# Waits of the weight-ternarising stage of a transformer layer on Trainium2: what the weight loads and the Abs pass wait for

## The chip, the cores and the metric

The kernel runs on all 8 cores of one Trainium2 chip, one batch entry of 2048 tokens on each. Each core has five engines with instruction streams of their own (TensorE, VectorE, ScalarE, GpSimd and SyncE, in the profile PE, DVE, ACT, POOL and SP) and 16 DMA engines. The metric is the device time in microseconds of the slowest core.

## The reference, cut to what matters

```python
def _bitlinear(x, w_latent):
    scale = clip(mean(abs(w_latent), axis=1, keepdims=True), 1e-05, None)
    tern = clip(round(w_latent / scale), -1.0, 1.0)
    w = w_latent + stop_gradient(tern - w_latent)
    return x @ (w * scale).T
h = _bitlinear(x, w_fc) + gate * (x @ v.T @ fast_b.T @ u.T)
r = maximum(h, 0.0)
return _bitlinear(r * r, w_proj)          # w_fc [4096, 1024], w_proj [1024, 4096]
# around it, x [8, 2048, 1024]:
x = x + attn_block(layernorm(x), ...)     # linear attention and a GELU MLP
x = x + ffn(layernorm(x), ...)            # the function above
```

Each row of w_fc and w_proj is thus replaced by its signs where the absolute value is above half of the row's mean absolute value, and by 0 elsewhere; the row's scale is applied later.

## The kernel before, in words

The program is written engine by engine with explicit semaphores. `block.sync`, `block.scalar`, `block.vector`, `block.tensor` and `block.gpsimd` append the given function's instructions to that engine's stream; no scheduler moves them. `b.inc` lets an instruction raise its engine's counter (`"t"`, `"v"`, `"s"` for TensorE, VectorE, ScalarE), `b.wait(engine, name, value)` makes an engine wait for a value, and `b.cnt[name]` is the count emitted so far. `b.dma` (L52) issues a transfer. Loads are issued by SP under the name `"ld"`, whose four semaphores are used in turn, and spills by GpSimd under `"gq"`, with two semaphores; each transfer also waits for the one before it on its own semaphore. Every engine's stream is in order.

The stages are: attention, output projection and GELU MLP (until about 3700 us), the statistics of the second layernorm, then the **weight stage** (from L1362 on, ends at L1562), a small stage that transposes `u` (L1603), and the second FFN over four groups of 512 tokens.

In the weight stage w_fc is taken in 32 stripes of 128 rows (loop at L1384), w_proj in 8 stripes of 128 rows by 4096 columns (loop at L1457).

A **w_fc stripe** `si` goes so. SP loads it (512 KB) in two halves into one of two buffers, `wfbuf[si % 2]` (L1388). ScalarE takes the absolute values into `ab_s` and their sum into `sc_fc` (L1399); in the profile this is a table load, the ACTIVATE and a read of the accumulator. VectorE forms scale and thresholds (four small instructions, L1408 to L1416), compares with the upper threshold into `ab_s` (L1419) and with the lower one into `tern_b` (L1422), which is the last reader of the buffer. TensorE transposes 8 blocks into `ps_trf` (L1432), VectorE copies them into one of two `evac_fc` buffers (L1444), and GpSimd spills these 256 KB to `spill_fc` in DRAM (L1450), as rows of 128 bf16 values. The tile names in the profile are `ph` for all f32 buffers of the stage (`wfbuf`, `ttf4`, `ab_s`, `abs4`) and `ph7b` for `tern_b` and the evacuation buffers.

A **w_proj stripe** `j` (2 MB) is loaded in four quarters into the single buffer `ttf4` (L1461), with rows of 1024 f32 values. ScalarE writes its absolute values to `abs4` (L1474). VectorE compares four quarters (L1496, L1499); the last of these eight instructions is the last reader of `ttf4`. Then four times: 8 transposes (L1512), a copy to one of two `evac_pj` buffers (L1523), a spill of 256 KB to `spill_pj` (L1530). The third copy waits for the first spill, whose buffer it takes, and the fourth for the second.

What the loads wait for is set by hand. The w_fc load waits for `vprev`, all VectorE work emitted before it, which is the copy of the stripe before:

```python
vprev = b.cnt["v"]
def _(sy, si=si, wb_=wb_, vprev=vprev):
    b.wait(sy, "v", max(vprev, v_ln0b))
```

The w_proj load waits for all VectorE work and for all spills emitted before it:

```python
b.wait(sy, "v", vprev)
b.wait(sy, "gq", gprev)
```

ScalarE waits only for the load (`"ld"`). Lines of helpers: DMAs are recorded at L57, waits at L81 and L83.

Of the kernel before, what the change touches and what calls it, by code (L numbers as in the profile page):

```python
# [85 lines left out]
def build_program(tap=None, phases=99):  # L86
# [29 lines left out]
    with contextlib.ExitStack() as ctx:  # L116
# [34 lines left out]
        b = Bld(nc, block)  # L151
# [25 lines left out]
        def emit_tap(src_ap):  # L177
            cv, cs, ct = b.cnt["v"], b.cnt["s"], b.cnt["t"]

            def _(gp):  # L180
                b.wait(gp, "v", cv)
                b.wait(gp, "s", cs)
                b.wait(gp, "t", ct)
                b.dma(gp, "gq", out=tap_d[0:src_ap.shape[0], 0:src_ap.shape[-1]],
                                   in_=src_ap)
                b.wait(gp, "gq")
            block.gpsimd(_)
# [3 lines left out]
        def _(sy):  # L191
            off = 0
            for nm in ["bo", "b2", "g1", "be1", "g2", "be2", "b1"]:
                nch = PC[nm][1]
                b.dma(sy, "ld", out=A_t[0:nch, off:off + 128],
                                   in_=bias_d[nm].rearrange("(c p) -> c p", p=128))
                off += 128
            b.dma(sy, "ld", out=gate_b[:], in_=gate_d.partition_broadcast(128))
            b.dma(sy, "ld", out=fbT[:], in_=fb_d)
            b.dma(sy, "ld", out=A_t[0:16, 1024:2048], in_=vw_d)  # L200
            b.dma(sy, "ld", out=ident[:], in_=ident_d)
        block.sync(_)
        ld_par = b.cnt["ld"]

        def _(v):
            v.memset(ones_c[:], 1.0)
            v.memset(epsc[:, 0:1], EPS_OUT)
            v.memset(epsc[:, 1:2], EPS_IN)
            b.inc(v.memset(ones_r[:], 1.0), "v", 1)
        block.vector(_)  # L210

        def _(sc):
# [4 lines left out]
        with nc.psum_tensor("ps_m", [128, 128], F32) as ps_m:  # L217
            off = 0
            for nm in ["bo", "b2", "g1", "be1", "g2", "be2", "b1"]:
                nch = PC[nm][1]  # L220
                vprev = b.cnt["v"]
# [20 lines left out]
            vprev = b.cnt["v"]  # L242
# [11 lines left out]
            for k in range(ND):  # L254
                vprev = b.cnt["v"]
# [21 lines left out]
        with nc.sbuf_tensor("ph0", [128, 5376], F32) as P0, \  # L277
# [9 lines left out]
            for si in range(NT):  # L287
                xb = xt[si % 2]
                wv_, ws_ = done[si - 2] if si >= 2 else (0, 0)
# [6 lines left out]
                ldv = b.cnt["ld"]  # L296
# [26 lines left out]
            vv = b.cnt["v"]  # L323
# [8 lines left out]
            sv = b.cnt["s"]  # L332
# [11 lines left out]
            for si in range(NT):  # L344
                xb, zb = xt[si % 2], zt[si % 2]
                wv_ = v_ev if si >= 2 else 0
# [5 lines left out]
                ldv = b.cnt["ld"]  # L352
# [727 lines left out]
        with nc.sbuf_tensor("ph5", [128, 9728], F32) as P5, \  # L1080
# [10 lines left out]
            for g in range(G):  # L1091
# [177 lines left out]
                with nc.psum_tensor(f"ps_sg1_{g}", [1, 512], F32) as psg1, \  # L1269
                     nc.psum_tensor(f"ps_sg2_{g}", [1, 512], F32) as psg2:  # L1270
                    for n in range(ND):
# [9 lines left out]
                        sv = b.cnt["s"]  # L1281
# [22 lines left out]
                    vv = b.cnt["v"]  # L1304
# [9 lines left out]
                    sv = b.cnt["s"]  # L1314
# [50 lines left out]
        v_ln0b = b.cnt["v"]  # L1365
# [14 lines left out]

        with nc.psum_tensor("ps_trf", [128, 1024], BF16) as ps_trf:
            g_fc = [0, 0]
            t_trf = 0
            for si in range(NF):  # L1384
                wb_ = wfbuf[si % 2]
                vprev = b.cnt["v"]

                def _(sy, si=si, wb_=wb_, vprev=vprev):  # L1388
                    b.wait(sy, "v", max(vprev, v_ln0b))
                    for hh in range(2):  # L1390
                        b.dma(sy, "ld", out=wb_[:, hh * 512:(hh + 1) * 512],
                              in_=wfc_d[si * 128:(si + 1) * 128,
                                        hh * 512:(hh + 1) * 512])
                block.sync(_)
                ldv = b.cnt["ld"]

                def _(sc, si=si, wb_=wb_, ldv=ldv):
                    b.wait(sc, "ld", ldv)
                    b.inc(sc.activation(ab_s, wb_, AF.Abs,  # L1399
                                        accum_out=sc_fc[:, si:si + 1]), "s", 1)  # L1400
                block.scalar(_)
                sv = b.cnt["s"]

                def _(v, si=si, wb_=wb_, sv=sv, t_trf=t_trf):
                    b.wait(v, "s", sv)
                    b.wait(v, "t", t_trf)
                    b.wait(v, "v")
                    b.inc(v.tensor_scalar(sc_fc[:, si:si + 1], sc_fc[:, si:si + 1],  # L1408
                                          INV_D, None, ALU.mult), "v", 1)
                    b.wait(v, "v")  # L1410
                    b.inc(v.tensor_scalar(sc_fc[:, si:si + 1], sc_fc[:, si:si + 1],
                                          1e-5, None, ALU.max), "v", 1)
                    b.wait(v, "v")
                    v.tensor_scalar(thr_s[:, 0:1], sc_fc[:, si:si + 1], 0.5,
                                    None, ALU.mult)
                    b.inc(v.tensor_scalar(thr_s[:, 1:2], sc_fc[:, si:si + 1], -0.5,  # L1416
                                          None, ALU.mult), "v", 1)
                    b.wait(v, "v")
                    b.inc(v.tensor_scalar(ab_s, wb_, thr_s[:, 0:1], None, ALU.is_gt),  # L1419
                          "v", 1)  # L1420
                    b.wait(v, "v")
                    b.inc(v.scalar_tensor_tensor(  # L1422
                        tern_b[:, 0:1024],
                        wb_, thr_s[:, 1:2], ab_s, ALU.is_lt, ALU.subtract), "v", 1)
                block.vector(_)
                vv = b.cnt["v"]

                def _(t, vv=vv):
                    b.wait(t, "v", vv)
                    last = None  # L1430
                    for k in range(ND):
                        last = t.transpose(ps_trf[:, k * 128:(k + 1) * 128],  # L1432
                                           tern_b[:, k * 128:(k + 1) * 128],
                                           ident_b[:])
                    b.inc(last, "t", 1)
                block.tensor(_)
                t_trf = b.cnt["t"]

                ev_ = evac_fc[si % 2]

                def _(v, t_trf=t_trf, gw=g_fc[si % 2], ev_=ev_):
                    b.wait(v, "t", t_trf)
                    b.wait(v, "gq", gw)
                    b.inc(v.tensor_copy(ev_, ps_trf[:]), "v", 1)  # L1444
                block.vector(_)
                vv = b.cnt["v"]

                def _(gp, si=si, vv=vv, ev_=ev_):
                    b.wait(gp, "v", vv)
                    b.dma(gp, "gq", out=sfc_d[si].transpose([1, 0, 2]),  # L1450
                                       in_=ev_
                                       .rearrange("p (k c) -> p k c", k=ND))
                block.gpsimd(_)
                g_fc[si % 2] = b.cnt["gq"]

            g_pj = [0, 0]
            for j in range(ND):  # L1457
                vprev = b.cnt["v"]
                gprev = b.cnt["gq"]

                def _(sy, j=j, vprev=vprev, gprev=gprev):  # L1461
                    b.wait(sy, "v", vprev)
                    b.wait(sy, "gq", gprev)
                    for qq in range(4):
                        b.dma(sy, "ld",
                              out=ttf4[:, qq * 1024:(qq + 1) * 1024],
                              in_=wpj_d[j * 128:(j + 1) * 128,
                                        qq * 1024:(qq + 1) * 1024])
                block.sync(_)
                ldv = b.cnt["ld"]  # L1470

                def _(sc, j=j, ldv=ldv):
                    b.wait(sc, "ld", ldv)
                    b.inc(sc.activation(abs4, ttf4, AF.Abs,  # L1474
                                        accum_out=sc_pj[:, j:j + 1]), "s", 1)
                block.scalar(_)
                sv = b.cnt["s"]
# [24 lines left out]
                            ALU.is_lt, ALU.subtract), "v", 1)  # L1502
                block.vector(_)
                vv = b.cnt["v"]

                for q in range(4):
                    def _(t, q=q, vv=vv):
# [28 lines left out]
            gprev = b.cnt["gq"]  # L1536
# [31 lines left out]
        with nc.sbuf_tensor("ph8", [128, 6672], F32) as P8, \  # L1568
# [32 lines left out]
            with nc.psum_tensor("ps_u", [128, 128], F32) as ps_u:  # L1601
                v_prev = v_prep
                for st in range(NF):  # L1603
# [7 lines left out]
                    vv = b.cnt["v"]  # L1611
# [18 lines left out]
            for g in range(G):  # L1630
# [20 lines left out]
                for k in range(ND):  # L1651
# [12 lines left out]
                    vv = b.cnt["v"]  # L1664
# [9 lines left out]
                with nc.psum_tensor(f"ps_lr_{g}", [16, 512], F32) as ps_lr:  # L1674
# [19 lines left out]
                    vv = b.cnt["v"]  # L1694
# [14 lines left out]
                with nc.psum_tensor(f"ps_h2_{g}", [128, 1536], F32) as ps_h2:  # L1709
# [4 lines left out]
                    for i in range(NF):  # L1714
                        ws_ = t_fc[i % 2]
# [7 lines left out]
                        ldv = b.cnt["ld"]  # L1723
# [51 lines left out]
                for half in range(2):  # L1775
                    with nc.psum_tensor(f"ps_y_{g}_{half}", [128, 2048], F32) as ps_y:
# [3 lines left out]
                        ldv = 0  # L1780
                        for i in range(NF):
                            if i % 2 == 0:
# [14 lines left out]
                                ldv = b.cnt["ld"]  # L1797
# [24 lines left out]
                        for jj in range(4):  # L1822
                            j = half * 4 + jj
# [82 lines left out]
```

How the kernel before makes its waits and increments, by code:

```python
    def dma(self, eng, base, out, in_, **kw):  # L52
        j = self.rri[base] % RR[base]
        self.rri[base] += 1
        s = f"{base}{j}"
        self.wait(eng, s)
        instr = eng.dma_start(out=out, in_=in_, **kw)
        instr.then_inc(self.sem[s], 16)
        self.cnt[s] += 16
        self.cnt[base] += 16
        self.snap[base][self.cnt[base]] = tuple(
            self.cnt[f"{base}{k}"] for k in range(RR[base]))
        return self.cnt[base]
# [1 line left out]
    def inc(self, instr, name, n=1):  # L65
        assert name not in self.snap
        instr.then_inc(self.sem[name], n)
        self.cnt[name] += n
        return self.cnt[name]
# [1 line left out]
    def wait(self, eng, name, val=None):  # L71
        if val is None:
            val = self.cnt[name]
        assert val <= self.cnt[name], \
            f"wait {name}>={val} but only {self.cnt[name]} emitted"
        if val == 0:
            return
        if name in self.snap:
            for k, c in enumerate(self.snap[name][val]):
                if c > 0:
                    eng.wait_ge(self.sem[f"{name}{k}"], c)
            return
        eng.wait_ge(self.sem[name], val)
```

## Time and profile before

| | us |
|---|---|
| three runs | 5910.05, 6027.0, 6244.59 (median 6027.0) |
| the profiled execution | 5910.97 |
| its span on the slowest core (core 3) | 5909.4 |
| spans of the 8 cores | 5900.5 to 5909.4 |
| mean granted clock of TensorE, all cores | 0.817 to 0.818 of full speed |
| TensorE busy (matmuls) | 3797.6 (64% of the span) |
| VectorE, ScalarE, GpSimd busy | 1589.7, 1224.8, 165.0 |

Busy times are those of instructions that compute; waiting, branches and the issue of DMAs don't count. The granted clock is a share of full speed: 1.00 is 2.4 GHz, 0.50 is 1.2 GHz. A timeline row gives the start, the duration, the engine with its line, what is written from what, and in brackets how long the engine was idle before and what ended that.

### The profile page before, as it was taken

What the parts mean: (1) busy time and instruction counts of PE and PEld (TensorE: products, weight loads), DVE (VectorE), ACT (ScalarE), POOL (GpSimd) and SP (SyncE); (2) the same over time, 40 slices, a digit from 0 to 9 for tenths busy, and PEclk for the clock granted to TensorE, in tenths of its full rate; (3) what the DMA queues carried; (4) which work ended last, traced back from release to release, by engine and by line L of the source; (5) the groups of instructions that cost most, each with busy time, mean ns of one, the idle gap of its engine ahead of it and who ended that gap; (6) DMA issues with size and microseconds to landing.
All of it is one profiled execution on the core that took longest, in us unless ns stands there. A gap on an engine that the chain in (4) does not pass through costs nothing.

```text
span 5909.4 us, 49644 instructions; the slowest of 8 cores (5900.5 to 5909.4 us)
## 1 busy us (share of the span) xinstructions
PE 3797.6 (64%) x16136; PEld 1605.1 (27%) x16136; DVE 1589.7 (27%) x1972; ACT 1224.8 (21%) x1279; POOL 165.0 (3%) x228
## 2 busy tenths in 40 slices
PE   1266654656965994994995996400013988969697
PEld 1122222222412441341441442000001333323233
DVE  2354555542014102202202201122333213031220
ACT  2034442320021202301301311222110504123050
POOL 0011110000000000000000000000010000000000
PEclk9988877866977996996997997755555999989799
DMA  2233331000002321431431431022221222212122
GB/s 94 93 114 107 105 109 47 1 0 29 0 0 64 93 86 47 89 100 32 100 93 37 96 93 43 18 66 69 75 87 36 54 68 47 61 49 59 50 54 68
DMA packets 655522, 374.36 MB, mean 63 GB/s; under 512 B 548176, under 2 KB 581152, under 8 KB 655280
## 3 DMA queue, kind: packets, MB, share of 16 engines
q1 hardware_dynamic: 635312, 304.06, 19.6%
q0 software_dynamic: 19968, 67.12, 3.4%
q8 instruction: 145, 2.38, 0.2%
q14 instruction: 97, 0.79, 0.1%
HBM read 312.39 MB, written 58.72 MB: 63 GB/s over the span
## 4 chain that ended last, share of the span: by engine, by line
PE 53%; DVE 19%; ACT 10%; DMA 10%; issue 6%; DVEq 1%; SPq 1%; ACTq 0%; POOLq 0%; POOL 0%
PE ps_p L1240 11%; PE ps_h L1178 11%; PE ps_h L1733 8%; PE ps_y L1812 8%; PE ps_wo L949 3%; DMA ph<-x 2%; PE ps_h L1736 2%; DMA ph<-wfc 2%; ACT L587 1%; DVE phwp L578 1%; DVE phwpb L594 1%; PE ps_ctx L902 1%; PE ps_s L991 1%; ACT phwpb L587 1%; PE ps_s L993 1%
## 5 line engine op out<-in xcount | busy, mean ns | idle before, releaser
L1178 PE MATMUL ps_h<-ph5p 128*128 128x512 bf16 x3072 | 682.2, 382 | 54.2 <-DVE ph5p L1140 35.8
L1240 PE MATMUL ps_p<-strB,ph5p 128*128 128x512 bf16 x3072 | 672.5, 382 | 32.4 <-DMA ph5p<-spill_w2p 32.1
L1812 PE MATMUL ps_y<-strB,ph8w 128*128 128x512 bf16 x2048 | 469.9, 388 | 63.3 <-DMA ph8w<-spill_pj 50.7
L1733 PE MATMUL ps_h<-ph8z,ph8w 128*128 128x512 bf16 x2048 | 473.9, 385 | 14.4 <-DMA ph8w<-spill_fc 14.4
L1178 PEld LDWEIGHTS ps_h<-ph5p 128*128 128x128 bf16 x3072 | 296.4, 98 | 439.6 <-issue 103.0
L1240 PEld LDWEIGHTS ps_p<-strB,ph5p 128*128 128x128 bf16 x3072 | 302.3, 99 | 402.6 <-issue 46.6
L501 PE MATMUL ps_v<-strB,ph1zp 128*128 128x512 bf16 x768 | 202.8, 433 | 272.1 <-DVE ph1zp L491 272.1
L1750 ACT ACT_TABLE_LOAD x128 | 164.2, 1283 | 955.2 <-PE ps_h L1736 935.0
L1194 ACT ACT_TABLE_LOAD x128 | 164.2, 1283 | 740.6 <-PE ps_h L1178 740.6
L1812 PEld LDWEIGHTS ps_y<-strB,ph8w 128*128 128x128 bf16 x2048 | 197.7, 99 | 336.9 <-issue 126.8
L501 PE MATMUL ps_q<-ph1qw,ph1zp 128*128 128x512 bf16 x768 | 199.8, 428 | 137.2 <-DVE ph1zp L491 137.2
L1733 PEld LDWEIGHTS ps_h<-ph8z,ph8w 128*128 128x128 bf16 x2048 | 192.2, 99 | 331.0 <-issue 124.9
L1432 PE MATMUL ps_trf<-ident_b,ph7b 128*128 128x128 bf16 x256 | 32.4, 306 | 351.3 <-DVE ph7b L1422 351.3
L1202 DVE CAST strB<-ps_h 128x512 bf16<-128x512 f32 x128 | 88.6, 692 | 526.8 <-ACT ps_h L1194 526.8
L1278 ACT ACT_TABLE_LOAD x32 | 41.1, 1283 | 845.0 <-DVE ph L1258 745.7
L1258 DVE TENSOR_SCALAR ph<-ps_p,pcol 128x512 f32<-128x512 f32 x32 | 21.4, 743 | 717.3 <-PE ps_p L1246 717.3
L949 PE MATMUL ps_wo<-strB,ph3w 128*128 128x512 bf16 x768 | 176.2, 387 | 50.1 <-DVE ph3w L474 31.9
L1761 DVE CAST strB<-ps_h 128x512 bf16<-128x512 f32 x128 | 88.6, 692 | 439.2 <-ACT ps_h L1753 439.2
L1512 PE MATMUL ps_trf<-ident_b,ph7b 128*128 128x128 bf16 x256 | 32.4, 306 | 263.5 <-DVE ph7b L1499 233.7
L501 PEld LDWEIGHTS ps_v<-strB,ph1zp 128*128 128x128 bf16 x768 | 82.1, 108 | 387.7 <-issue 320.7
L501 PE MATMUL ps_k<-strB,ph1zp 128*128 128x512 bf16 x768 | 168.4, 379 | 0.0
L1828 DVE SCALAR_TENSOR_TENSOR ph<-ps_y,scn_pj,strA 128x512 f32<-128x512 f32 x32 | 21.8, 744 | 505.1 <-PE ps_y L1812 505.1
(209 smaller groups left out, 3703.9 us busy)
## 6 DMA issues: line engine op xcount, KB each, us to landing
ph5p<-spill_w1p SPq DMA_DIRECT2D x256, 256.0 KB
ph5p<-spill_w2p SPq DMA_DIRECT2D x256, 256.0 KB
ph8w<-spill_fc SPq DMA_DIRECT2D x128, 256.0 KB
ph8w<-spill_pj SPq DMA_DIRECT2D x128, 256.0 KB
ph<-x SPq DMA_DIRECT2D x32, 512.0 KB
phwp<-w1t SPq DMA_DIRECT2D x32, 512.0 KB
spill_w1p<-phwpb POOLq DMA_DIRECT2D x64, 256.0 KB, 4.5
phwp<-w SPq DMA_DIRECT2D x32, 512.0 KB
```

The source lines that it names most:

```text
L501: last = t.matmul(ps[:, cols], zz[:, k * 128:(k + 1) * 128], ww.rearrange("p (k w) -> p k w", k=ND)[:, k, cols], start=(pi == 0 and k == 0 ...
L587: b.inc(sc.copy(wpb[:, 0:1024], tb), "s", 1)
L949: t.matmul(ps_wo[:, cols], wfn[:, e_, n * 128:(n + 1) * 128], bfn(e_)[:, cols], start=(pi == 0 and e_ == 0), stop=False)
L1178: last = t.matmul(dst, ww[:, k * 128:(k + 1) * 128], aa[:, k, :], start=(pi == 0 and k == 0), stop=(pi == 2 and k == ND - 1))
L1194: b.inc(sc.activation(ps_h[:, 1024:1536], src, AF.Gelu, bias=pc("b1", i)), "s", 1)
L1202: b.inc(v.tensor_copy(B16[:, i * 1024:i * 1024 + 512], ps_h[:, 1024:1536]), "v", 1)
L1240: last = t.matmul(ps_p2[:, n * 512:(n + 1) * 512], ww[:, n * 128:(n + 1) * 128], mm, start=(i == 0 and pi == 0), stop=False)
L1733: t.matmul(dst, fcb[i % 2][:, k * 128:(k + 1) * 128], zz(k), start=(pi == 0 and k == 0), stop=False)
L1736: b.inc(t.matmul(dst, uTg[:, i * 128:(i + 1) * 128], t2T[0:16, :], start=False, stop=True), "t", 1)
L1750: b.inc(sc.activation(bcz[:, 0:512], src, AF.Relu, scale=scn_fc[:, i:i + 1]), "s", 1)
L1761: b.inc(v.tensor_copy(B16[:, i * 1024:i * 1024 + 512], ps_h2[:, 1024:1536]), "v", 1)
L1812: last = t.matmul(ps_y[:, jj * 512:(jj + 1) * 512], buf[:, off + jj * 128:off + (jj + 1) * 128], mm, start=(i == 0 and pi == 0), stop=(i = ...
```

## The change

The order of all instructions stays; the waits of the stage's loads and of its Abs passes are set anew.

- The w_fc load waits for the last comparison (`v_fcg`) and the Abs (`s_fcg`) of the stripe that used the same buffer, two stripes earlier, and no longer for the copy of the stripe before.
- The w_proj load waits for the last comparison of the stripe before (`v_pjt`; for the first stripe, the last w_fc copy), and no longer for copies and spills.
- ScalarE's Abs waits, besides the load, for all VectorE work emitted before it (`vprev_abs`), that is for the copy of the stripe before, in both loops. `ab_s` and `tern_b` are still single buffers.

```diff
             g_fc = [0, 0]
+            v_fcg = [0, 0]
+            s_fcg = [0, 0]
...
-                vprev = b.cnt["v"]
-
-                def _(sy, si=si, wb_=wb_, vprev=vprev):
-                    b.wait(sy, "v", max(vprev, v_ln0b))
+
+                def _(sy, si=si, wb_=wb_, wv_=v_fcg[si % 2], ws_=s_fcg[si % 2]):
+                    b.wait(sy, "v", max(wv_, v_ln0b))
+                    b.wait(sy, "s", ws_)
...
-                def _(sc, si=si, wb_=wb_, ldv=ldv):
+                vprev_abs = b.cnt["v"]
+
+                def _(sc, si=si, wb_=wb_, ldv=ldv, vprev_abs=vprev_abs):
                     b.wait(sc, "ld", ldv)
+                    b.wait(sc, "v", vprev_abs)
...
                 sv = b.cnt["s"]
+                s_fcg[si % 2] = sv
...
                 vv = b.cnt["v"]
+                v_fcg[si % 2] = vv
...
             g_pj = [0, 0]
+            v_pjt = b.cnt["v"]
             for j in range(ND):
-                vprev = b.cnt["v"]
-                gprev = b.cnt["gq"]
-
-                def _(sy, j=j, vprev=vprev, gprev=gprev):
-                    b.wait(sy, "v", vprev)
-                    b.wait(sy, "gq", gprev)
+
+                def _(sy, j=j, v_pjt=v_pjt):
+                    b.wait(sy, "v", v_pjt)
...
-                def _(sc, j=j, ldv=ldv):
+                vprev_abs = b.cnt["v"]
+
+                def _(sc, j=j, ldv=ldv, vprev_abs=vprev_abs):
                     b.wait(sc, "ld", ldv)
+                    b.wait(sc, "v", vprev_abs)
...
                 vv = b.cnt["v"]
+                v_pjt = vv
```

How the waits of SP's stream stand where w_fc goes over into w_proj, before (`vs`, `ss` are the counters of VectorE and ScalarE, `ld0` to `ld3` and `gq0`, `gq1` those of loads and spills; L57 is the helper that issues):

```order
L57 DMA ph<-wfc 128x512 [waits vs,ld0]
L57 DMA ph<-wfc 128x512 [waits ld1]
L1469 UNCONDITIONAL_BRANCH
L57 DMA ph<-wpj 128x1024 [waits vs,gq0,gq1,ld2]
L57 DMA ph<-wpj 128x1024 [waits ld3]
L57 DMA ph<-wpj 128x1024 [waits ld0]
L57 DMA ph<-wpj 128x1024 [waits ld1]
```

The same place after:

```order
L57 DMA ph<-wfc 128x512 [waits vs,ss,ld0]
L57 DMA ph<-wfc 128x512 [waits ld1]
L1473 UNCONDITIONAL_BRANCH
L57 DMA ph<-wpj 128x1024 [waits vs,ld2]
L57 DMA ph<-wpj 128x1024 [waits ld3]
L57 DMA ph<-wpj 128x1024 [waits ld0]
L57 DMA ph<-wpj 128x1024 [waits ld1]
```

The instructions stand as they stood; the w_fc load has a second counter to wait for, and the w_proj load has lost the two of the spills. On ScalarE, the Abs of w_fc and of w_proj before:

```order
L1399 ACTIVATE ph,sc_fc<-ph 128x1024 [waits ld0,ld1,ld2,ld3]
L1401 UNCONDITIONAL_BRANCH
L1399 ACTIVATE ph,sc_fc<-ph 128x1024 [waits ld0,ld1,ld2,ld3]
...
L1474 ACTIVATE ph,sc_pj<-ph 128x4096 [waits ld0,ld1,ld2,ld3]
```

and after:

```order
L1403 ACTIVATE ph,sc_fc<-ph 128x1024 [waits ld0,ld1,ld2,ld3,vs]
L1405 UNCONDITIONAL_BRANCH
L1403 ACTIVATE ph,sc_fc<-ph 128x1024 [waits ld0,ld1,ld2,ld3,vs]
...
L1481 ACTIVATE ph,sc_pj<-ph 128x4096 [waits ld0,ld1,ld2,ld3,vs]
```

Here VectorE's counter has come in as a fifth, and last, wait.

## Rows read from the trace of the kernel before

**Rows 1.** Windows by stage, core 3: length, busy times, clock, DMA share, GB/s

```profile
core 3: us, PE busy (x) PEld busy (x) DVE busy (x) ACT busy (x) POOL busy (x), PEclk, DMA share, GB/s
0.00:3804.20 3804.20, 2580.16 (x10992) 1090.09 (x10992) 1067.24 (x1105) 778.00 (x775) 99.67 (x148) 0.85 0.23 65
3804.20:4180.00 375.80, 32.36 (x256) 24.75 (x256) 104.08 (x224) 77.81 (x96) 28.39 (x32) 0.50 0.21 67
4180.00:4475.50 295.50, 32.38 (x256) 24.77 (x256) 91.54 (x128) 39.94 (x24) 28.35 (x32) 0.50 0.29 85
...
4522.00:5909.40 1387.40, 1140.78 (x4601) 462.67 (x4600) 309.27 (x445) 329.10 (x384) 8.56 (x16) 0.90 0.23 55
4720.00:4860.00 140.00, 121.46 (x536) 53.00 (x536) 9.08 (x11) 0.00 (x0) 1.11 (x2) 0.94 0.27 65
4860.00:4900.00 40.00, 10.58 (x36) 4.50 (x36) 22.52 (x35) 0.00 (x0) 1.06 (x2) 0.55 0.06 26
```

**Rows 2.** Timeline of the last w_fc stripe (start us, us, engine, line)

```profile
4163.55 0.69 DVE L1444 COPY ph7b<-ps_trf 128x1024 bf16<-128x1024 bf16 x1 [1.40 <-PE ps_trf L1432]
4164.37 0.80 SPq L57 DMA_DIRECT2D ph<-wfc  x2
4164.84 0.89 POOL L57 DMA_DIRECT2D spill_fc<-ph7b  x1 [10.82 <-DVE ph7b L1444]
4168.04 1.28 ACT L1399 ACT_TABLE_LOAD   x1 [9.12 <-DMA ph<-wfc]
...
4172.43 1.29 DVE L1422 SCALAR_TENSOR_TENSOR ph7b<-ph 128x1024 bf16<-128x1024 f32 x1
...
4175.12 0.69 DVE L1444 COPY ph7b<-ps_trf 128x1024 bf16<-128x1024 bf16 x1 [1.40 <-PE ps_trf L1432]
```

**Rows 3.** Table loads ahead of both Abs: ns min/median/max, first and last start

```profile
L1399 ACT ACT_TABLE_LOAD  x32: 1283/1283/1283, 3807.7 to 4168.0; - x32
...
L1474 ACT ACT_TABLE_LOAD  x8: 1283/1283/1283, 4190.0 to 4447.9; - x8
```

**Rows 4.** Timeline of w_proj: the first load, then the second stripe

```profile
4179.70 2.19 SPq L57 DMA_DIRECT2D ph<-wpj  x4
...
4228.04 1.28 ACT L1474 ACT_TABLE_LOAD   x1 [33.00 <-DMA ph<-wpj]
...
4241.73 1.28 DVE L1499 SCALAR_TENSOR_TENSOR ph7b<-ph 128x1024 bf16<-128x1024 f32 x1
...
4245.71 0.89 POOL L57 DMA_DIRECT2D spill_pj<-ph7b  x1 [30.53 <-DVE ph7b L1523]
...
4249.04 0.69 DVE L1523 COPY ph7b<-ps_trf 128x1024 bf16<-128x1024 bf16 x1 [1.83 <-DMA spill_pj<-ph7b]
...
4251.14 0.69 DVE L1523 COPY ph7b<-ps_trf 128x1024 bf16<-128x1024 bf16 x1 [1.40 <-DMA spill_pj<-ph7b]
...
4255.74 2.32 SPq L57 DMA_DIRECT2D ph<-wpj  x4
...
4266.06 1.28 ACT L1474 ACT_TABLE_LOAD   x1 [33.01 <-DMA ph<-wpj]
```

**Rows 5.** Timeline ahead of the stage: VectorE hands over to a table load

```profile
3796.18 2.28 DVE L1006 SCALAR_TENSOR_TENSOR rows<-ps_s,rows 1x2048 f32<-1x2048 f32 x1
3798.59 1.28 ACT L1015 ACT_TABLE_LOAD   x1 [16.23 <-DVE rows L1006]
```

**Rows 6.** DMA issues of the stage: KB each, median us to landing

```profile
spill_fc<-ph7b POOLq DMA_DIRECT2D x32, 256.0 KB, 3.8
spill_pj<-ph7b POOLq DMA_DIRECT2D x32, 256.0 KB, 3.2
```

**Rows 7.** Timeline of the first w_fc load

```profile
3804.14 0.81 SPq L57 DMA_DIRECT2D ph<-wfc  x2
3807.67 1.28 ACT L1399 ACT_TABLE_LOAD   x1 [3.78 <-DMA ph<-wfc]
```

**Rows 8.** Windows: a w_proj load, and the copies with their four spills

```profile
4218.50:4228.00 9.50, 0.00 (x0) 0.00 (x0) 0.00 (x0) 0.00 (x0) 0.00 (x0) 0.50 0.66 221
4205.00:4217.50 12.50, 4.04 (x32) 3.09 (x32) 2.79 (x5) 0.00 (x0) 3.55 (x4) 0.50 0.35 84
```

## The prediction

> **What bounds the kernel now.** I read the stages first, by cutting the span into windows [rows 1]. TensorE is busy 2580.2 of 3804.2 us before the weight stage and 1140.8 of 1387.4 us after it. Between them lie 671 us in which it works for 65 us: 375.8 us for the w_fc stripes and 295.5 us for the w_proj stripes. VectorE is busy 104.1 and 91.5 us there, ScalarE 77.8 and 39.9, and the DMA engines 21% and 29% of the time. No engine is near full, so this stage is a chain of single steps, each waiting for the one before. All of the diff lies in it; nothing outside has to be counted, unless the clock of the stage behind changes (last rival).
>
> Then one w_fc stripe in order of time [rows 2]. The evacuation copy of a stripe ends at 4164.24 (4163.55 + 0.69). SP issues the next load at 4164.37, and ScalarE starts at 4168.04: 3.80 us in which all engines but the spill's issue stand still. From there the stripe needs 7.77 us until its own copy ends (4175.12 + 0.69 = 4175.81). The first and last of the 32 table loads at L1399 are 360.3 us apart [rows 3]: 31 periods of 11.62 us, of which 7.77 are work, so the wait is 3.85 us in the mean.
>
> One w_proj stripe in the same way [rows 4]. ScalarE starts at 4228.04; VectorE ends its last comparison, the last reader of the stripe, at 4243.01 (call this T); the fourth copy ends at 4251.83 (T+8.8); SP issues the next load only at 4255.74 (T+12.7), since it also waits for the last spill; ScalarE starts again at 4266.06 (T+23.05). The mean period is (4447.9 − 4190.0)/7 = 36.84 us [rows 3]; less the 14.97 us from ScalarE's start to T it leaves 21.87 us after T, and less the 12.73 us until the issue, 9.14 us for the load of 2 MB, from issue to ScalarE's start.
>
> **The change part by part.** No instruction is added, removed or put elsewhere; only waits differ, as the order shows.
>
> 1. w_fc loads. Load si no longer waits for the copy of stripe si−1, but for the last comparison and the Abs of stripe si−2. The comparison ends at 4173.72 in [rows 2] (4172.43 + 1.29), 2.1 us before its own copy ends, and the load is wanted one whole stripe after that. With a new period of about 7.9 us it is issued some 10 us ahead, and needs 3.7 us (4164.37 to 4168.04). So it is off the path. SP's other new wait, for ScalarE of si−2, is met 4 us earlier and costs nothing; behind SP stands only the next load.
>
> 2. The new wait of ScalarE. It must wait for the copy of stripe si−1, all VectorE work so far. This keeps the chain serial: the table load, the Abs, the comparisons, the transposes and the copy still follow one another. What is left of the 3.85 us is a hand-over from VectorE to ScalarE. [Rows 5] have one: VectorE ends at 3798.46, the table load begins at 3798.59, 0.13 us. Behind the waiting Abs only the next Abs is queued. The new period is 7.77 + 0.13 = 7.90 us; 31 × (3.85 − 0.13) = 115 us. Bounds: if five waits instead of four cost a further 0.2 us each time, 109; 31 × 3.85 = 119 if the hand-over costs nothing.
>
> 3. w_proj loads. They now wait for T alone, not for the copies or the spills. The load is issued at T+0.13 and, undisturbed, ScalarE could start at T+9.3 (0.13 + 9.14). The copies end at T+8.8, and ScalarE waits for them too, so without contention the load still ends last: 21.87 − 9.27 = 12.6 us per stripe, 7 stripes, 88 us. But three spills now run beside the load. The trace has no such overlap with a load this long. The near cases: a w_fc spill, which runs beside a load of 0.5 MB, lands in 3.8 us in the median, against 3.2 for w_proj spills, which run beside none [rows 6]. The loads hardly notice: 3.67 us beside a spill in [rows 2], 3.53 for the very first one, beside none [rows 7]. During a w_proj load the DMA engines are busy for 0.66, and for the 12.5 us of copies and spills 0.35 [rows 8], which is 1.1 us of all 16 for each spill; three spills are 3.3 us of work, and 34% of 9.5 us, 3.2 us, are free. I take 1 to 2 us of delay for the gate of ScalarE, that is T+11.0: 21.87 − 11.0 = 10.9 us, 7 times: 76 us.
> The bad end: the first spill, issued at T+2.7 (4245.71), moves on only row by row while the load lasts and lands after it, at about T+12.5. The third copy waits for that spill (its idle time of 1.83 us in [rows 4] is already such a wait) and ends 0.7 us after it, and the fourth copy ends 2.1 us after the third (4249.04 to 4251.14). ScalarE then starts at about T+15.5 and a stripe gains 6.4 us: 45 us. Of the two ends, 45 and 88, the rows on mild contention lie nearer to the upper.
>
> 4. The first w_proj load. Before, it waited for the last w_fc spill and was issued at 4179.70 [rows 4]; now it waits for the copy that ended at 4175.81. It is issued 3.8 us earlier and runs beside one spill: 3 us gained (bounds 2 and 4).
>
> 5. The first two w_fc loads are issued together; the first may land up to 0.5 us later. I count nothing.
>
> What is late next: in the w_fc loop the chain through ScalarE and VectorE itself; in the w_proj loop the load and the copies almost together.
>
> Sum: 115 + 76 + 3 = 194 us. The profiled execution took 5910.97 us: 5717 us. That execution equals the fastest of the three runs; their median is 6027 and the slowest 6245. I predict a run like the profiled one and let the upper side of the range take in some of this spread. What a measurement of this kernel can tell from no change is about 2%, 118 us.
>
> How the chip shares its DMA engines decides between 76 and 45. [Rows 6] show a spill 0.6 us longer beside a load, no more. The Trainium skill, page "DMA: Bandwidth & Descriptors", section "Queues, rings and completion order", says that each DMA engine goes round its queues packet by packet, and drains a packet of some 9 to 17 descriptors before it turns to the next. By that rule a spill of many small rows needs few turns, and is not held until the load is through; the trace agrees as far as the 0.6 us go. By a rule of one descriptor in turn, a spill with 64 rows of 256 B per engine would outlast the load's 32 rows of 4 KB; that is the first rival.
>
> **Rivals.**
> (a) Spills starve beside the load (the bad end above). For it: a spill is cut into small rows, and the third copy waited 1.83 us for one even with no load beside it. Against it: the 0.6 us of [rows 6]. 115 + 45 + 3 = 163 us, 5748 us.
> (b) The table load leaves the path: if its place is ahead of the new wait, 1.28 us go from each of 31 + 7 stripes, 49 us more, 5668 us. Against it: at [rows 5] and at each Abs it starts only after the wait.
> (c) The w_fc prefetch does not happen, because something still holds the load behind the copy (SP's queue is in order, and each load waits for the one two stripes ahead on its own semaphore). Then only 76 + 3 remain: 5832 us, within 2%. Against it: those loads landed long before.
> (d) Slower: TensorE's clock in the last stage. The weight stage is granted 0.50 (1.2 GHz), the dense halves of the last stage 0.94, the gaps in it 0.55 [rows 1]; the clock follows what the engine did before. If the stage were granted 0.70 in the mean instead of 0.90, its 1140.8 us of busy time would grow by 1140.8 × (0.90/0.70 − 1) = 326 us, 6043 us. It decides from a mean of 0.77 down, where 194 us are used up. Against it: the engine's work in that stage and the pause ahead of it are the same, and the clock came back after each gap.
>
> **How the numbers follow.** The forecast has 0.72 (its own range 5700 to 5735, from 88 and 60 us in the w_proj loop); (a) 0.13, (b) 0.05, (c) 0.07, (d) 0.03. Faster by over 2%: forecast, (a) and (b), 0.90; within 2%: (c), 0.07; slower: (d), 0.03. The range goes down to (b), 5665, and up past (a) and (c), and past the forecast with the 116 us by which the median of the three runs stood above the profiled one (5833), to 5865.
>
> **What would show it.** In the profile after: table loads at the w_fc Abs 7.9 us apart and put down to VectorE's copy, not to the DMA; the stretch from the first w_fc load to the first w_proj load some 257 us long (3.5 + 32 × 7.9) instead of 376; w_proj table loads 26 us apart (14.97 + 11.0) instead of 36.84; the w_proj spill's time to landing between 3.2 and 5 us, over 8 if (a) is right; a clock of 0.90 in the last stage. The forecast is wrong if the w_fc table loads still wait for DMA, or if the w_proj period is over 29 us.

## The result, and the profile after

| | before | after |
|---|---|---|
| median of ten runs, us | 6083.07 | 5774.87 |
| lowest to highest | 5910.05 to 6244.59 | 5730.03 to 6188.8 |
| the profiled execution | 5910.97 | 5733.13 |
| its span, slowest core | 5909.4 (core 3) | 5731.6 (core 1) |

In some executions of either kernel the cores of one die run at a lower clock for a while; the ratios compare undisturbed runs only, and of e5 and e8, whose profiled executions were of that kind, the undisturbed die's rows are read and no time is used. The ratio is 0.9658, with a 95% interval of 0.9532 to 0.9783: faster. A later comparison on one chip (e9 below) gives 0.9694, with a narrower interval of 0.9675 to 0.9713. The profiled executions differ by 177.8 us, where 194 were forecast.

The windows by stage after, core 1 (length, busy time and count of each engine, granted clock, DMA share, GB/s), against [rows 1]:

```profile
core 1: us, PE busy (x) PEld busy (x) DVE busy (x) ACT busy (x) POOL busy (x), PEclk, DMA share, GB/s
0.00:3803.40 3803.40, 2583.85 (x10992) 1090.56 (x10992) 1067.37 (x1105) 777.99 (x775) 99.65 (x148) 0.85 0.23 65
3803.40:4059.00 255.60, 32.35 (x256) 24.73 (x256) 104.09 (x224) 77.83 (x96) 27.66 (x32) 0.50 0.34 98
4059.00:4289.80 230.80, 32.38 (x256) 24.77 (x256) 91.54 (x128) 39.93 (x24) 29.08 (x33) 0.50 0.36 110
4336.50:5731.60 1395.10, 1142.78 (x4600) 464.60 (x4600) 309.17 (x445) 329.12 (x384) 8.56 (x16) 0.90 0.23 55
```

VectorE is busy 104.09 and 91.54 us in the two loops, as before; only idle time has gone, 375.8 to 255.6 and 295.5 to 230.8 us. The last stage is granted 0.90 as before. It is 8 us longer on this core than on core 3 of before. That is a difference between cores: what lies outside the two loops takes 5262 to 5276 us on the eight cores after and 5265 to 5274 before, by each core's span less the stretch from its first w_fc to its last w_proj table load.

The table loads ahead of the two Abs passes (ns min/median/max, first and last start), against [rows 3], from core 3, the core of those rows:

```profile
L1403 ACT ACT_TABLE_LOAD  x32: 1283/1283/1283, 3803.3 to 4046.9; - x32
...
L1481 ACT ACT_TABLE_LOAD  x8: 1283/1283/1283, 4064.9 to 4257.9; - x8
```

The w_fc period is (4046.9 − 3803.3)/31 = 7.86 us (11.62 before), the w_proj period (4257.9 − 4064.9)/7 = 27.57 us (36.84 before). A w_fc stripe in order of time, core 1, against [rows 2]:

```profile
3961.90 8.64 SPq L57 DMA_DIRECT2D ph<-wfc  x4
3963.13 0.69 DVE L1450 COPY ph7b<-ps_trf 128x1024 bf16<-128x1024 bf16 x1 [1.40 <-PE ps_trf L1438]
3963.89 1.28 ACT L1403 ACT_TABLE_LOAD   x1 [5.39 <-DVE ph7b L1450]
...
3970.97 0.69 DVE L1450 COPY ph7b<-ps_trf 128x1024 bf16<-128x1024 bf16 x1 [1.40 <-PE ps_trf L1438]
3971.74 1.28 ACT L1403 ACT_TABLE_LOAD   x1 [5.40 <-DVE ph7b L1450]
```

The copy ends at 3963.82 and the table load begins at 3963.89, 0.07 us later, where 3.80 us of load stood before. The load for a stripe further on is issued at 3961.90, ahead of the copy. The same for the end of the first w_proj stripe and the start of the second, against [rows 4]:

```profile
4058.39 1.95 SPq L57 DMA_DIRECT2D ph<-wpj  x4
...
4068.91 1.28 ACT L1481 ACT_TABLE_LOAD   x1 [15.97 <-DMA ph<-wpj]
...
4082.60 1.29 DVE L1506 SCALAR_TENSOR_TENSOR ph7b<-ph 128x1024 bf16<-128x1024 f32 x1
...
4084.02 29.07 SPq L57 DMA_DIRECT2D ph<-wpj  x8
...
4086.44 0.89 POOL L57 DMA_DIRECT2D spill_pj<-ph7b  x1 [26.70 <-DVE ph7b L1531]
...
4093.28 0.69 DVE L1531 COPY ph7b<-ps_trf 128x1024 bf16<-128x1024 bf16 x1 [5.48 <-DMA spill_pj<-ph7b]
...
4095.37 0.69 DVE L1531 COPY ph7b<-ps_trf 128x1024 bf16<-128x1024 bf16 x1 [1.40 <-PE ps_trf L1520]
4096.14 1.28 ACT L1481 ACT_TABLE_LOAD   x1 [22.23 <-DVE ph7b L1531]
```

The comparisons end at T = 4083.89, and the next load is issued 0.13 us later. The first spill goes out at 4086.44, and the third copy, which needs its buffer, starts only at 4093.28, after 5.48 us of waiting for it (1.83 in [rows 4]). The spill landed 6.7 us after its issue instead of 3.2, and ScalarE starts at T+12.25.

The records of DMA packets show where these 3.5 us go. A line gives a queue, its packets, their MB, and their time as a share of the time of the 16 engines; q1 carries SP's loads, q0 GpSimd's spills. The first line is the kernel before, core 3, from 4247.1 to 4249; the next is the changed kernel, core 1, from 4087.9 to 4090.9, and the last two are the same core from 4090.9 to 4093.2:

```profile
q0 software_dynamic: 80, 0.26, 57.8%
...
q1 hardware_dynamic: 317, 1.13, 98.9%
...
q1 hardware_dynamic: 131, 0.48, 52.6%
q0 software_dynamic: 123, 0.44, 50.7%
```

In the kernel before, the first packet of a spill starts 1.4 us after the issue (none before 4247.1, for the spill of 4245.71 in [rows 4]). In the changed kernel it starts only after 4.5 us. From the time when it could have started, 4087.9, the load's packets take 98.9% of the engines' time. Once the spill's packets have started, both queues have about half each, and the load isn't over when the spill lands: 24 of its packets start after 4093.2. Over all eight cores, seven such spills on each, the first packet starts 4.0 to 5.0 us after the issue, and the landing lies between 1.4 us before and 1.5 us after the end of the load's last packet. So the spill is kept out for some 3 us more than before and then shares the engines with the load; below, "held" means this. The spill's 1024 rows of 256 B go as 64 packets of 4 KB (and 16 of 4 bytes).

The waits in the stage, core 1 (who waited for whom, us in total, times, longest):

```profile
ACT L1403 <- DVE ph7b L1450: 162.1, 30, 5.8
ACT L1481 <- DVE ph7b L1531: 158.2, 7, 24.0
```

Before, all these waits of ScalarE ended on a load. Now all but three of the 40 end on a copy.

### The profile page after: what moved, and what is told of

The parts are those of the page before. It is cut to its first block, busy times and chain, and to the rows that moved or that the text cites. A ratio compares the mean times of both kernels' runs of the same rounds, so it can differ in the third digit from the quotient of the medians.

```text
span 5731.6 us, 49698 instructions; the slowest of 8 cores (5714.9 to 5731.6 us)
## 1 busy us (share of the span) xinstructions
PE 3803.2 (66%) x16136; PEld 1607.5 (28%) x16136; DVE 1589.8 (28%) x1972; ACT 1224.9 (21%) x1279; POOL 165.0 (3%) x228
## 4 chain that ended last, share of the span: by engine, by line
PE 54%; DVE 20%; ACT 9%; DMA 9%; issue 6%; DVEq 1%; SPq 0%; ACTq 0%; POOLq 0%; POOL 0%
PE ps_p L1240 12%; PE ps_h L1178 11%; PE ps_h L1741 8%; PE ps_y L1820 7%; PE ps_wo L949 3%; DMA ph<-x 2%; PE ps_h L1744 2%; DMA ph8w<-spill_pj 1%; ACT L587 1%; DVE phwp L578 1%; DVE phwpb L594 1%; PE ps_s L991 1%; PE ps_ctx L902 1%; ACT phwpb L587 1%; PE ps_s L993 1%
```

## The experiments

The periods are differences of first and last table load, as above; "the stretch" runs from the first w_fc load to the load of `u` (671.4 us before, 486.4 after on core 1). Chips differ a little: the fastest run of the kernel before is 5891.4 us beside e1 to e4, 5909.8 beside e5 to e7, 5906.9 beside e8 and e9.

### e1: only the w_fc half

The w_proj loop is put back to that of the kernel before:

```diff
-                def _(sy, j=j, v_pjt=v_pjt):
-                    b.wait(sy, "v", v_pjt)
+                def _(sy, j=j, vprev=vprev, gprev=gprev):
+                    b.wait(sy, "v", vprev)
+                    b.wait(sy, "gq", gprev)
...
-                    b.wait(sc, "v", vprev_abs)
```

(the last line in the w_proj loop alone).

> Only the w_fc half of the change; the w_proj loop is that of the kernel before. If the parts simply add, as in the sum of the prediction: the w_fc table loads are 7.86 us apart (11.62 before), the w_proj ones 36.8; the stretch from the first w_fc load to the load of u is 671 - 117 = 554 us, the time 5911 - 117 = 5794 us. The rival, that a faster w_fc loop gives part of its gain back later (spills still under way at the first w_proj load, clock of the last stage), expects a stretch of over 560 us or a last stage longer than the 1387 us of before.

```profile
L1403 ACT ACT_TABLE_LOAD  x32: 1283/1283/1283, 3797.2 to 4040.8; - x32
...
L1480 ACT ACT_TABLE_LOAD  x8: 1283/1283/1283, 4060.7 to 4312.5; - x8
```

On core 3, the slowest, the periods are 7.86 and 35.97 us, and the stretch 4340.2 − 3793.2 = 547 us, 7 less than expected, since core 3's w_proj loads were slower in the first profile than those of any other core (36.84 against 35.99 to 36.29 us). Median 5782.69 us, ratio 0.9805 (0.9782 to 0.9827), an interval with the prediction's limit of 2% in it. The fastest run, 5779.9, is 111 us under this chip's 5891.4. In the mean of the eight cores the stretch is 547.8 us, 117 less than the 665.2 of before, and from the load of `u` to the end it takes 1433.0 us instead of 1434.6. So nothing is given back later: the w_fc half gains its 117 us on a core, and 111 between the slowest cores of two executions.

### e2: only the w_proj half

The w_fc loop is put back in the same way:

```diff
-                def _(sy, si=si, wb_=wb_, wv_=v_fcg[si % 2], ws_=s_fcg[si % 2]):
-                    b.wait(sy, "v", max(wv_, v_ln0b))
-                    b.wait(sy, "s", ws_)
+                def _(sy, si=si, wb_=wb_, vprev=vprev):
+                    b.wait(sy, "v", max(vprev, v_ln0b))
...
-                    b.wait(sc, "v", vprev_abs)
```

> Only the w_proj half. If the parts add: w_fc table loads 11.62 us apart, w_proj ones 27.6, stretch 671 - 68 = 603 us, time 5843 us. If the w_proj half depends on the w_fc half, its period differs from 27.6 by over 0.5 us.

The periods are 11.61 and (4367.4 − 4174.7)/7 = 27.53 us on core 7, 11.55 to 11.68 and 27.21 to 27.70 over the cores; the stretch is 603.1 us, as expected (601.1 in the mean of the cores, 64 less than before). Median 5845.67 us, ratio 0.9903 (0.9866 to 0.9941), within 2%; the fastest run, 5826.2, is 65 us under this chip's fastest of before. The halves don't depend on each other, 111 + 65 = 176 us.

### e3: four evacuation buffers in the w_proj loop

```diff
-            g_pj = [0, 0]
+            g_pj = [0, 0, g_fc[0], g_fc[1]]
+            evac4 = evac_pj + evac_fc
...
-                    ev_ = evac_pj[q % 2]
+                    ev_ = evac4[q]
```

with `g_pj[q]` for `g_pj[q % 2]`, so that no copy waits for a spill of its own stripe.

> The changed kernel with four evacuation buffers in the w_proj loop, so that no copy waits for a spill of its own stripe. Theory A (a spill that is issued while the load is queued lands only when the load is through, and the load itself is hardly slowed): the copies end at T+8.8, the gate of ScalarE is T+9 to T+10, the w_proj period 24 to 25 us instead of 27.6, the stretch 486 - 22 = 464 us; some of ScalarE's waits are now put down to the load. Theory B (spills and load share the DMA engines, and both are slowed): the load is late as well, ScalarE waits for it until T+11.5 or more, the period stays above 26.5 us.

The timeline of core 6, second stripe; its last comparison ends at T = 4100.07:

```profile
4100.21 1.75 SPq L57 DMA_DIRECT2D ph<-wpj  x4
...
4102.77 0.89 POOL L57 DMA_DIRECT2D spill_pj<-ph7b  x1 [16.40 <-DVE ph7b L1532]
...
4104.86 0.89 POOL L57 DMA_DIRECT2D spill_pj<-ph7b  x1 [1.21 <-DVE ph7b L1532]
...
4107.76 0.69 DVE L1532 COPY ph7b<-ps_trf 128x1024 bf16<-128x1024 bf16 x1 [1.40 <-PE ps_trf L1521]
4110.07 1.28 ACT L1482 ACT_TABLE_LOAD   x1 [19.98 <-DMA ph<-wpj]
4110.75 1.76 POOL L57 DMA_DIRECT2D spill_pj<-ph7b  x2 [5.00 <-DMA spill_pj<-ph7b]
```

The copies are over at 4108.45 (T+8.4), and ScalarE waits for the load until T+10.0. The first spill landed 7.5 us after its issue, at 4110.2, where the load's last packet ended at 4109.3; in the stripe before it landed at 4083.8, 0.5 us ahead of that packet. From issue to ScalarE's start the load takes 9.86 us here and 9.42 in the mean of all stripes of the eight cores, against 8.40 in the kernel before, which had no spill beside it (9.04 on core 3, whose loads were the slowest). So the load loses 1.0 us and the first spill 3.6 (6.8 in the mean, instead of 3.2). The periods are 24.07 to 25.06 us, and one run took 5696.15 us, 195 under this chip's fastest of before. Theory A has the gate and the period: what set the gate was that the copies waited for a spill of their own stripe. Its picture of that spill is right in the outcome alone, a landing at about the load's end: the spill's first packet starts 3.9 to 4.8 us after the issue, beside the load's packets.

### e4: half of the load

```diff
-                    for qq in range(4):
+                    for qq in (range(4) if j == 0 else range(2)):
```

> The changed kernel, in which the w_proj stripes from the second on load only the first two of their four quarters (1 MB instead of 2; the other half of the stripe keeps old data, so the output is not the reference's). Theory A: the load is through at about T+5.5, the first spill, issued at T+2.6, lands at that time or at its undisturbed 3.2 us after its issue, whichever is later, so at T+5.8; the third copy waits no more than in the kernel before, the gate is T+9, the period 24 us. Theory B: the spill is slowed in proportion for as long as it runs beside the load and lands 4.5 us or more after its issue, the gate is T+10 or later, the period over 25 us.

The periods are 24.00 to 24.81 us on the eight cores. The slowest spill lands in 3.7 to 5.0 us instead of 6.6 to 8.2, and ScalarE still waits for the copies. The first packet of the first spill now starts 1.4 to 2.1 us after the issue, so with 1 MB of load the hold is all but gone. But 3.7 to 5.0 is not the 3.2 that theory A gave; on core 6 the third copy still waits 3.69 us. What is left there is sharing. The spill was issued at 4104.16; the first line is from 4104.1 to 4105.7, the other two from 4105.7 to 4107:

```profile
q1 hardware_dynamic: 157, 0.58, 92.9%
...
q0 software_dynamic: 61, 0.22, 52.4%
q1 hardware_dynamic: 66, 0.20, 39.1%
```

The load's last packet ended at 4106.92, T+5.5 as expected (T = 4101.46), and the spill landed only at 4109.2. The periods are theory A's, the slowest landings (over 4.5 us) theory B's: each has a part, A's the 3 us of hold, B's the sharing after it. One run took 5703.0 us.

### e5: each quarter of the load waits only for its own quarter

```diff
-                    b.wait(sy, "v", v_pjt)
                     for qq in range(4):
+                        b.wait(sy, "v", v_pjq[qq])
...
-                v_pjt = vv
+                v_pjq = [vv - 6, vv - 4, vv - 2, vv]
```

> The changed kernel, two evacuation buffers as there, but each quarter of the w_proj load waits only for the comparison of its own quarter of the stripe before, so the load starts 6.8 us before T and is through at about T+3. Theory A (spills are held while a load is queued): with the load through early, the first spill, issued at T+2.6, lands at T+6 or T+7, the copies end at T+9, the gate is T+9 and the w_proj period 14.97 + 9 = 24 us. If what delayed the third copy was something else than the load (the spill's own queue, GpSimd), the period stays at 27.5 us. A third way: the load reads from DRAM at the same rate but now beside VectorE's comparisons, and if these were slowed by it the stretch from ScalarE's start to T would be longer than 14.97 us.

The rows are of core 5. The last comparison ends at T = 4079.18:

```profile
4081.73 0.89 POOL L57 DMA_DIRECT2D spill_pj<-ph7b  x1 [25.28 <-DVE ph7b L1531]
...
4085.31 0.69 DVE L1531 COPY ph7b<-ps_trf 128x1024 bf16<-128x1024 bf16 x1 [2.22 <-DMA spill_pj<-ph7b]
...
4087.40 0.69 DVE L1531 COPY ph7b<-ps_trf 128x1024 bf16<-128x1024 bf16 x1 [1.40 <-PE ps_trf L1520]
4088.17 1.28 ACT L1481 ACT_TABLE_LOAD   x1 [18.97 <-DVE ph7b L1531]
```

The first spill lands 3.4 us after its issue, ScalarE starts at T+9.0, and the period is 24.10 us (24.10 to 24.27 over all cores). The load isn't through at T+3: its last quarter can't be issued before T, and its last packet ends at T+4.1 to T+4.9 on cores 4 to 7. So the spill, issued at T+2.6, is not held although load is still under way beside it; the hold goes with the amount of load that is queued when the spill is issued. ScalarE's start to T is 4079.18 − 4064.20 = 14.98 us: the comparisons aren't slowed by the load beside them. This gains 3.4 us per stripe, where e3 gained some 2.9 by another way, the buffers instead of the order of the transfers.

### e6: the Abs of w_fc apart from VectorE

```diff
                     b.wait(sc, "ld", ldv)
-                    b.wait(sc, "v", vprev_abs)
-                    b.inc(sc.activation(ab_s, wb_, AF.Abs,
+                    b.wait(sc, "s")
+                    b.inc(sc.activation(abs4[:, 0:1024], wb_, AF.Abs,
```

> The changed kernel, in which the w_fc Abs writes to a buffer of its own (abs4, not used in that loop) and waits only for its load and for ScalarE's own earlier work, not for VectorE. If the new wait of ScalarE is what still binds the w_fc loop, ScalarE's 2.8 us (table load, Abs, accumulator) leave the chain and the period falls from 7.86 to 5.0 to 5.2 us; 31 periods give 84 us. The rival: the loads (512 KB each, with 256 KB of spill per stripe, 150 GB/s at that pace) become the bound, then ScalarE waits for DMA and the period stays above 6 us.

The period is (3978.4 − 3811.2)/31 = 5.39 us (5.39 to 5.43 over the cores): 2.45 us less, 76 us in all instead of 84. One run took 5659.92 us, 73 under the changed kernel's 5733.13 (on another chip; the fastest run of the kernel before took 5909.8 us on this one and 5910.05 on that). So the added wait is what binds the w_fc loop after the change. ScalarE now waits for loads (96.5 us in 31 waits), but ahead of VectorE, which doesn't stand still for it: the loop runs at the pace of VectorE and the transposes. The missing 8 us lie for the most part in a row of its own, the comparison L1424 (L1419 before):

```profile
L1403 ACT ACT_TABLE_LOAD  x32: 1283/1283/1283, 3811.2 to 3978.4; - x32
...
L1424 DVE TENSOR_SCALAR ph<-ph x32: 753/1026/1079, 3814.7 to 3983.2; 128x1024 f32<-128x1024 f32 x32
```

### e7: all of it together

Quarter loads, four buffers, and both Abs passes without a wait for VectorE.

> Quarter loads, four evacuation buffers, and both Abs passes without a wait for VectorE (w_fc into abs4). w_fc period 5.1 us; w_proj: VectorE's comparisons and copies follow one another, the Abs (5.1 us) lies beside the copies, so a stripe takes 9.7 us of comparisons and 8.9 us of copies, 18.6 us instead of 27.6. Against the changed kernel 31 x 2.75 + 7 x 9 = 148 us less: about 5570 us where the changed kernel takes 5715 to 5733 (chips differ by 0.3%). If spills are held by the early loads here too, the w_proj period is over 20 us.

Median 5607.28 us (5605.79 to 5619.23), ratio 0.9474 (0.9455 to 0.9492), against 0.9694 for the changed kernel (e9): it beats the kernel before and the changed one, but 5607 is not the 5570 expected. The w_fc period is 5.41, the w_proj period 20.46 us on core 1 (19.90 to 20.46 over the cores), not 18.6. The waits show why, core 1:

```profile
ACT L1481 <- DMA ph<-wpj: 123.9, 8, 16.4
```

ScalarE, free of the copies, waits for the load: at the longest, on core 1, until T+6.4 (4048.38 after a comparison that ended at 4041.94), in the mean of all cores until T+5.1, and not T+3, for the reason found in e5: the last quarter goes out only at T. The 5.1 us of ScalarE then end after the copies.

### e8: spills of long rows

```diff
-                        dst = spj_d[j // 4, q * ND:(q + 1) * ND, j % 4]
-                        b.dma(gp, "gq", out=dst.transpose([1, 0, 2]),
-                                           in_=ev_
-                                           .rearrange("p (i c) -> p i c", i=ND))
+                        dst = spj_d[j // 4].rearrange("i jj p c -> (i jj p c)") \
+                            .rearrange("(r p f) -> r p f", p=128, f=1024)
+                        b.dma(gp, "gq", out=dst[(j % 4) * 4 + q], in_=ev_)
```

> The changed kernel, whose w_proj spills write the same 256 KB as 128 rows of 2 KB instead of 1024 rows of 256 B (to one contiguous stretch of spill_pj each, so the blocks stand in the wrong order there and the output is not the reference's). Both readings of what holds the first spill: (row by row) the DMA engines take one row of the load and one of the spill in turn; then a spill needs 8 turns per engine instead of 64, is not held by the load, and lands 3 to 5 us after its issue: copies end at T+9, the gate moves to the load at T+10, the w_proj period falls from 27.5 to 25 us or less. (held) the spill waits for the load to get through whatever its rows are; then it lands at T+9 as before and the period stays at 27 us or more.

Core 1:

```profile
4091.19 0.56 POOL L57 DMA_DIRECT2D spill_pj<-ph7b  x1 [26.03 <-DVE ph7b L1531]
...
4097.97 0.69 DVE L1531 COPY ph7b<-ps_trf 128x1024 bf16<-128x1024 bf16 x1 [5.43 <-DMA spill_pj<-ph7b]
```

Undisturbed, such a spill lands in 2.3 us (3.2 with short rows). Here the third copy starts 6.8 us after the spill's issue, at T+9.3, as in the changed kernel, and the period is 27.49 us. The length of the spill's rows doesn't matter; it is held. But this edit didn't change what the DMA engines take in turn: by the packet records a spill of long rows, too, goes as 64 packets of 4 KB. What other packets would do is not shown.

### e9: the changed kernel again

No edit; five rounds beside the kernel before, on one chip.

> The changed kernel as it is, once more, timed in five rounds beside the kernel before on one chip, for the size of the whole. If the two halves add (111 us from the fast spans of e1, 65 from e2), it is 176 to 180 us faster, a ratio of 0.970; by the prediction's sum of 194 us it would be 0.967. Its w_fc period 7.86 us and w_proj period 27.5 us are as in its first profile.

The periods are 7.85 to 7.86 and 27.27 to 27.67 us over the cores. Median 5733.56 us (fastest 5726.97), ratio 0.9694 (0.9675 to 0.9713). The fastest runs differ by 5906.9 − 5727.0 = 180 us. The sum of the halves fits; the prediction's 0.967 lies just below the interval.

## Why the prediction was right or wrong

**w_fc loop, 115 us: right.** Core 3 gives 31 × (11.62 − 7.86) = 117 us. The load is off the path, ScalarE waits for the copy alone, and the hand-over costs 0.07 us instead of 0.13. A fifth wait costs nothing measurable. (SP's wait for the Abs is met 3.2 us ahead of the one for the comparison, not 4, and costs nothing either.) e6 shows that this wait is what is late next.

**w_proj loop, 76 us: the load is issued early as forecast, but the delay was taken too small, and the gate is another.** It is 7 × (36.84 − 27.57) = 65 us on core 3 and 61 in the mean of the eight cores (36.20 and 27.50), within the bounds of 45 and 88. From T to ScalarE's start it takes 12.6 us in the mean (27.57 − 14.97), where I took 11.0. The step that failed is the 1 to 2 us of delay for ScalarE's gate, with its reason that 34% of the DMA engines' time is free and that "the rows on mild contention lie nearer to the upper" end. The 0.66 of [rows 8] is a mean over a stretch with idle ends. In the middle of that same load the engines had no room (core 3 before; the last two figures are DMA share and GB/s):

```profile
4221.00:4224.00 3.00, 0.00 (x0) 0.00 (x0) 0.00 (x0) 0.00 (x0) 0.00 (x0) 0.50 0.94 306
4224.00:4226.00 2.00, 0.00 (x0) 0.00 (x0) 0.00 (x0) 0.00 (x0) 0.00 (x0) 0.50 0.98 399
```

[Rows 6] could not show it either: there a spill met only the last 3 us of a short load. Beside a load of 2 MB the spill is held and lands at about the load's end (e3); with half of the load queued, or most of it sent earlier, it is hardly held (e4, e5), and the length of its rows doesn't matter (e8). The gate itself was another than the sum had: not the load but the copies, since the third waits for the first spill (e3, with more buffers, gives 24.6 us in the mean of the cores instead of 27.5). That is the chain of rival (a), which the forecast was wrong to set aside. Rival (a)'s size was wrong instead: it had the spill creep along row by row and land after the load, at T+12.5. It lands at T+9.3 in the mean, since it gets about half of the engines' time once its packets have started, while the load goes on. So 65 us, and not 45.

**What the rule of turns made of it.** In the after profile the first spill landed after 6.7 us. The Trainium skill, page "DMA: Bandwidth & Descriptors", section "Queues, rings and completion order", has each DMA engine go round its queues packet by packet, from which I took it that a spill isn't held. The trace agrees with the rule for the second half of the spill's time, in which the two queues have 52.6% and 50.7% of the engines. It disagrees with my reading for the first 4.5 us, in which the spill has no packet at all. Rival (a)'s own picture, one row in turn, falls too: 8 long rows per engine took as long as 64 short ones (e8), and both are 4 packets per engine beside the load's 32. GpSimd's issue is no longer than before, 0.89 us. What keeps the first packet out for 3 us, and why 2 MB of queued load does it and 1 MB hardly does, stays open.

**The first w_proj load, 3 us: right.** From the last w_fc to the first w_proj table load it is 22.0 us before and 18.0 after on core 3 (4190.0 − 4168.0, 4064.9 − 4046.9), 4 us; in the mean of the eight cores 20.9 and 17.6, 3.3 us.

**The sum.** 117 + 65 + 4 = 186 us on core 3 against 194. The times differ by less, 178 us in the profiled runs, since another core is now the slowest: core 3 owed its place before partly to its slow w_proj loads, and these are off the path. The mean of the eight cores is the better measure: the stretch goes from 665.2 to 485.1 us, 180 us.

**The other rivals.** (b) fell: the table load begins after the wait (3963.89). (c) fell: no w_fc table load but the first ones waits for a load. (d) fell: the last stage is granted 0.90.

**The level, where the forecast's range failed.** The profiled run after, 5733.13, is 16 us above the forecast of 5717, and the median of ten runs, 5774.87, 58 us above it. Both lie in the range. But the ratio of 0.9658 applied to the ten-run median of before, 6083.07, is 5875 us, 10 us past its upper end. The step that failed there is the last one of the sum, "let the upper side of the range take in some of this spread": I took three runs' median, 116 us above the profiled run, for the kernel's level, while that of ten is 172 above. Three runs had not shown the level.

## What to carry to other kernels

When a load is moved ahead so that it runs beside a store, ask who waits for the store: here the load hid as planned, and a copy that needed the store's buffer became the gate. Either give the store's source more buffers (e3) or send the load off in parts as its buffer comes free, so that little of it is still queued when the store is issued (e5). And don't read room for a store from the mean DMA share of a load: look at the middle of it. And where a prefetch needs a new wait to keep a scratch buffer safe, look for an unused buffer first: the wait cost 2.45 us in each of 31 stripes (e6).

## What was not expected

A spill issued 2.4 us after a load of 2 MB sends its first packet 4.5 us after its issue instead of 1.4, and lands after 6.7 us instead of 3.2, at about the time when the load does; the load takes 1.0 us more (e3). With rows of 2 KB instead of 256 B the spill lands after 6.8 us instead of 2.3.

In e6 the comparison over 128 x 1024 f32 takes 1.03 us in the median instead of 0.75 (minimum 0.753), where it falls on GpSimd's issue of a spill. The timeline shows both orders, core 5:

```profile
3955.72 0.89 POOL L57 DMA_DIRECT2D spill_fc<-ph7b  x1 [4.58 <-DVE sc_fc L1416]
3956.07 1.03 DVE L1424 TENSOR_SCALAR ph<-ph 128x1024 f32<-128x1024 f32 x1
...
3961.53 0.75 DVE L1424 TENSOR_SCALAR ph<-ph 128x1024 f32<-128x1024 f32 x1
3961.61 1.15 POOL L57 DMA_DIRECT2D spill_fc<-ph7b  x1 [5.01 <-DVE ph L1421]
```

Where GpSimd has begun, VectorE's instruction is 0.28 us longer; where VectorE has begun first, it takes its 0.75 and GpSimd's issue up to 1.15 instead of 0.89. On the eight cores of e6, 229 of 256 comparisons begin during an issue, and 1.03 us is their median; the other 27 take 0.75. In the changed kernel no comparison falls on an issue, and all 256 take 0.75. The Trainium skill, page "SBUF — State Buffer", section "SBUF: two separate sides", says that VectorE in some modes and GpSimd share a port pair, that the first to start holds it for its whole instruction, and that the other is blocked. The two orders agree with it in who is delayed, but not in by how much: blocked to the end of the issue at 3956.61, the comparison above would have been 0.54 us late and not 0.28. No experiment moved the issue alone, so that the overlap costs the time is shown by these rows, and that the port is the cause is not shown. It costs 6.8 us of the w_fc loop in the mean of the cores, most of the 8 that e6 missed.
